# Two-layer transformer on one core: attention in float32 row strips, with q and k moved to their strips by one transfer per head and chunk, in place of stacked bfloat16 parts read back from DRAM

## The reference

```python
# layer 0: q, k, v: [16 heads, 2048, 8]; q and k are rotated (rope); k and v come from a latent of 32
q = apply_rope(q); k = apply_rope(k)
scores = jnp.einsum('bhqd,bhkd->bhqk', q, k) / jnp.sqrt(jnp.float32(HEAD_DIM))
scores = jnp.where(causal[None, None], scores, -jnp.inf)
attn = jax.nn.softmax(scores, axis=-1)
out = jnp.einsum('bhqk,bhkd->bhqd', attn, v)
```

## Time and profile before

| | us |
|---|---|
| median of 3 runs | 1527.86 |
| lowest and highest of them | 1524.72 and 4729.34 |
| span of the profiled execution | 1517.5 |
| attention, layer 0 | 109.8 to 605.3 |
| attention, layer 1 | 815.9 to 1308.3 |

### The profile page before, as it was taken

The page is one execution under the profiler, slowest core; times in us unless marked ns, Lnnn a source line. Parts: engine busy times, 40 slices in busy tenths (PEclk is TensorE's granted clock), DMA queues, the critical chain, the costliest instruction groups (busy, mean ns, idle before and its releaser), DMA issues. The chain is left out here.

```text
span 1517.5 us, 20983 instructions
## 1 busy us (share of the span) xinstructions
PE 1211.4 (80%) x7346; PEld 524.4 (35%) x7347; DVE 951.7 (63%) x2598; ACT 683.7 (45%) x895; POOL 187.9 (12%) x257
## 2 busy tenths in 40 slices
PE   2917999999799998319553899999989999676984
PEld 2502333333233343207421223233333334444663
DVE  6627888888678772301163788888868775342443
ACT  1302465665566666103230445566656667421331
POOL 4110000000000000344410000000000000054442
PEclk9857999999899999559875899999999999777997
DMA  4154000230502000022216310140120000011113
GB/s 128 31 118 68 16 16 15 39 74 16 67 15 73 3 3 1 22 63 57 76 50 123 52 43 19 35 87 25 26 44 2 3 3 2 1 35 43 47 47 104
DMA packets 41740, 64.10 MB, mean 42 GB/s; under 512 B 5440, under 2 KB 27872, under 8 KB 41328
## 3 DMA queue, kind: packets, MB, share of 16 engines
q1 hardware_dynamic: 37328, 53.95, 16.4%
q0 software_dynamic: 4320, 8.92, 1.7%
HBM read 45.55 MB, written 18.92 MB: 42 GB/s over the span
## 5 line engine op out<-in xcount | busy, mean ns | idle before, releaser
L792 ACT ACTIVATE probs_at<-st 128x1024 f32<-128x1024 f32 (+3 forms) x640 | 545.7, 897 | 382.4 <-PE st L747 236.4
L810 DVE TENSOR_REDUCE mxp_at<-mx 128x1 f32<-128x512 f32 x768 | 498.4, 685 | 96.0 <-PE mx L716 95.1
L716 PE MATMUL mx<-ks,qs 128*128 128x512 bf16 (+3 forms) x1280 | 379.9, 368 | 84.9 <-DVEq L801 33.2
L747 PE MATMUL st<-qs,ks 128*128 128x512 bf16 (+3 forms) x1280 | 355.6, 354 | 13.9 <-DMA qs<-shrow_at 12.6
L812 DVE CUSTOM_DVE_ANT_0 junk_at<-mx,maskN 128x384 f32<-128x384 f32 (+3 forms) x512 | 241.2, 485 | 104.7 <-PE mx L716 102.4
L763 PE MATMUL av<-probs_at,vs 128*32 128x512 f32 (+3 forms) x2560 | 301.7, 543 | 0.2
L716 PEld LDWEIGHTS mx<-ks,qs 128*128 128x128 bf16 x1280 | 104.8, 98 | 437.7 <-DVE mxp_at L810 183.6
L747 PEld LDWEIGHTS st<-qs,ks 128*128 128x128 bf16 x1280 | 123.4, 99 | 111.0 <-ACT probs_at L792 21.8
L1027 POOL DMA_INDIRECT perm<-rows,pos x64 | 63.3, 989 | 512.6 <-SPq L1136 248.4
L750 PE MATMUL st<-maskTb,identb 128*128 128x128 bf16 x512 | 100.9, 222 | 0.0
L763 PEld LDWEIGHTS av<-probs_at,vs 128*32 128x32 f32 x2560 | 50.6, 108 | 107.2 <-issue 96.7
(11 more groups left out here) (232 smaller groups left out, 1027.8 us busy)
## 6 DMA issues: line engine op xcount, KB each, us to landing
qs<-q_parts SPq DMA_DIRECT2D x63, 128.0 KB
ks<-k_parts SPq DMA_DIRECT2D x18, 384.0 KB
w_sb<-in_w_dram SPq DMA_DIRECT2D x16, 256.0 KB, 3.1
q_parts<-part_pj SPq DMA_DIRECT2D x12, 256.0 KB, 3.0
k_parts<-part_pj SPq DMA_DIRECT2D x12, 256.0 KB, 4.7
perm<-in_pad_dram SPq DMA_DIRECT2D x1, 2600.0 KB, 11.6
rows_f<-perm SPq DMA_DIRECT2D x39, 65.0 KB, 1.8
ks<-k_parts SPq DMA_DIRECT2D x12, 192.0 KB
```

The costliest lines, as they stand in the source:

```text
L716: pe.matmul(buf[:, 0:w], QS[p][:, j, (4 * Q + qb) * P:(4 * Q + qb + 1) * P], KS[p][:, j, c * CH:c * CH + w], start=True, stop=True).then_i ...
L747: mm = pe.matmul(st[half][:, y, off:CH], KS[p][:, j, kb * P:(kb + 1) * P], QS[p][:, j, Q * CH + off:(Q + 1) * CH], start=True, stop=True, ...
L792: act.activation(probs[:, s % 2, 2 * half:2 * half + 2, off:CH], st[half][:, :, off:CH], ACT.Exp, scale=SCALE).then_inc(exp_done[half], 1)
L810: ins = v.tensor_reduce(dst, buf[:, 0:w], AX.X, ALU.max)
```

## The change

- q and k stay float32. QT and KT hold all 16 heads: head 4g + j lies in partitions 32j to 32j + 7 of plane g. Partition 32j + 8 of KT holds ones, that of QT the shift. The split in three parts, the DRAM tensors, `load_q`, `load_k` and all waits on them are gone.
- `project` writes each chunk flat into qf (one operation in layer 1, by ScalarE for q and by VectorE for k; rope's last operation in layer 0). SP then issues, for each chunk and each of q and k, sixteen transfers of one head (8 partitions x 512 columns) from qf to the head's strip: 128 a layer. The block ends when all have landed.
- Maxima are float32 products over 8 rows and scores over 9 rows, each in the 32-row strip of its head (`tile_position=(32j, 0)`). The mask stays bfloat16 over the whole array and comes after both heads of a half.
- v goes straight into VS for all heads (copied by ScalarE in project); GpSimd's copies are gone.
- Probs has three buffers. The units come in another order, the maxima with the head innermost, each rotating buffer has a semaphore of its own. The copies of "turn" and "attT" go from VectorE to ScalarE; the shift is no longer split.
- The planner is new: it keeps a time per strip, charges w/1200 us for a product of w columns, and writes ScalarE's order too.

```diff
-UNITS = [(0, 0), (0, 1), (0, 2), (1, 1), (0, 3), (1, 2), (1, 3), (1, 0),
-         (2, 2), (2, 3), (3, 3), (2, 1), (3, 1), (2, 0), (3, 0), (3, 2)]
+UNITS = [(g, Q) for Q in (1, 0, 2, 3) for g in range(NG - 1)] + [(NG - 1, Q) for Q in (3, 2, 1, 0)]
...
-    return [(g, Q, j, qb, c) for qb in range(TPC) for j in range(GH) for c in range(Q + 1)]
+    return [(g, Q, j, qb, c) for qb in range(TPC) for c in range(Q + 1) for j in range(GH)]
...
+        found = []
+        if chores:
+            t, kind, x = min(chores)
+            found.append((max(pe, t, all_rows, free[b] + lat) - .2, "chore"))
+        if s < NST and ready[UNIT[s]] is not None and s < a + PB:
+            found.append((max(pe, ready[UNIT[s]] if STEPS[s][2] == 0 else 0., exp_done[half] + lat, rows[2 * half], rows[2 * half + 1]) - .1, "scores"))
+        if a < NST and probs_ready[a] is not None:
+            found.append((max(pe, probs_ready[a] + lat, all_rows, av_free + lat if STEPS[a][2] == 0 else 0.), "values"))
+        if k < len(maxes):
+            found.append((max(pe, rows[maxes[k][1][2]], free[b] + lat), "max"))
+        t, what = min(found)
+        if what == "max":
+            u, x = maxes[k]
+            w = max_width(x)
+            pe = max(t, pe) + .03
+            rows[x[2]] = pe + w / 1200
+            dve = max(dve, rows[x[2]] + lat) + .08 + w * .00104
...
+        elif what == "scores":
+            off = step_off(s)
+            pe = max(t + .1, pe) + .06
+            rows[2 * half] = rows[2 * half + 1] = done = pe + (CH - off) / 1200
+            if on_diagonal(s):
+                pe = done = max(rows) + .2
+                rows = [done] * GH
+            act = max(act, done + lat) + .05 + 2 * (CH - off) * .000833
...
+        elif what == "values":
+            pe = max(t, pe)
+            rows = [pe + (CH - step_off(a)) / 1200 + .05] * GH
...
                 for n, (i, c) in enumerate(steps):
...
+                    sp.wait_ge(flat_ready[i], s4 + c + 1)
+                    for h in range(H):
+                        g, j = divmod(h, GH)
+                        sp.dma_start((m.QT, m.KT)[i][RT * j:RT * j + HD, g, cols(c)], qf[i][h * HD:(h + 1) * HD, cols(c)]).then_inc(m.sem(f"heads_in{c}"), 16)
+                for c in range(NC4):
+                    sp.wait_ge(m.sem(f"heads_in{c}"), 16 * 2 * H * (L + 1))
...
-                        pe.matmul(buf[:, 0:w], QS[p][:, j, (4 * Q + qb) * P:(4 * Q + qb + 1) * P],
-                                  KS[p][:, j, c * CH:c * CH + w], start=True, stop=True).then_inc(mx_ready, 1)
+                        pe.matmul(buf[:, 0:w], QT[row(j, HD), g, (4 * Q + qb) * P:(4 * Q + qb + 1) * P], KT[row(j, HD), g, c * CH:c * CH + w],
+                                  start=True, stop=True, tile_position=(RT * j, 0)).then_inc(mx_ready, 1)
...
                         j = 2 * half + y
-                        mm = pe.matmul(st[half][:, y, off:CH], KS[p][:, j, kb * P:(kb + 1) * P], QS[p][:, j, Q * CH + off:(Q + 1) * CH],
-                                       start=True, stop=True, skip_group_check=diag)
-                        if diag:
+                        mm = pe.matmul(st[half][:, y, off:CH], KT[row(j, HD + 1), g, kb * P:(kb + 1) * P],
+                                       QT[row(j, HD + 1), g, Q * CH + off:(Q + 1) * CH], start=True, stop=True, tile_position=(RT * j, 0),
+                                       skip_group_check=on_diagonal(s))
+                    if on_diagonal(s):
+                        for y in range(2):
                             mm = pe.matmul(st[half][:, y, off:off + P], m.identb[:], m.maskTb[:], start=False, stop=True, skip_group_check=True)
                     mm.then_inc(st_ready[half], 1)
```

More of the change, by code:

```diff
@@ L73, in step_off, with on_diagonal @@
     return max(0, STEPS[s][2] * P - STEPS[s][1] * CH)
+def on_diagonal(s):
+    return STEPS[s][2] >= TPC * STEPS[s][1]
 def schedule():
[L79 to L95, removed]
+    maxes = [(u, m) for u, (g, Q) in enumerate(UNITS) for m in max_tiles(g, Q)]
+    last_max = [max(k for k, (x, _) in enumerate(maxes) if x == u) for u in range(NU)]
+    lat = .15
+    pe = dve = act = 0.
+    rows = [0.] * GH
+    free = [0.] * MXBUF
+    exp_done, probs_ready = [0., 0.], [None] * NST
+    ready, evacuated = [None] * NU, [None] * NU
@@ L96, in schedule @@
+    av_free = 0.
     normed = [0] * NC4
-    while k < len(base) or s < NST or norms:
+    chores = []
+    pe_order, act_order, rot = [], [], []
+    k = s = half = a = 0
+    while k < len(maxes) or s < NST or a < NST or chores:
         b = len(rot) % MXBUF
[L99 to L102, removed]
-            free[b] = dve
-            out.append(("rot", len(rot)))
-            rot.append((kind, x))
[L106 to L157, removed]
@@ L162 @@
+    return pe_order, act_order, rot, (pe, act, dve)
+PE_ORDER, ACT_ORDER, ROT, _ = schedule()
 NROT = len(ROT)
-ATTT_AT = {x: k for k, (kind, x) in enumerate(ROT) if kind == "attT"}
-NORM_AT = {x: k for k, (kind, x) in enumerate(ROT) if kind == "norm"}
+AT = {x: k for k, x in enumerate(ROT)}
+USES = [len(range(b, NROT, MXBUF)) for b in range(MXBUF)]
+TURN_NO = {x: n for n, x in enumerate(x for kind, x in ROT if kind == "turn")}
 class Count:
@@ L333, in project @@
         hT = sb("hT", [P, T])
-        qf, res = [sb(f"qf{i}", [P, CH]) for i in range(2)], [sb(f"res{i}", [P, CH]) for i in range(2)]
-        parts = [[sb(f"part{i}{a}", [P, T], BF) for a in range(3)] for i in range(2)]
+        qf = [sb(f"qf{i}", [P, T]) for i in range(2)]
         xn = sb("xn", [P, TILES, D])
@@ L728, in rotate @@
                         mm.then_inc(mx_ready, 1)
[L729 to L730 removed]
+                    else:
+                        pe.wait_ge(*released(AT["attT", x]))
                         for qb in range(TPC):
@@ L765, in values @@
                     mm.then_inc(av_done, 1)
-                for item in ORDER:
+                for item in PE_ORDER:
                     if item[0] == "rot":
                         rotate(item[1])
-                    elif item[0] == "av":
+                    elif item[0] == "values":
                         values(item[1])
                     else:
-                        _, s, half = item
-                        if STEPS[s][2] == 0 and half == 0:
-                            u = UNIT[s]
-                            pe.wait_ge(shift_set[u % 4], 16 * (L * (NU // 4) + u // 4 + 1))
-                        scores(s, half)
+                        scores(item[1], item[2])
@@ L779, in _, with exponent @@
             @block.scalar
             def _(act):
+                def exponent(s, half):
+                    off = step_off(s)
+                    if half == 0 and SB + s >= PB:
+                        act.wait_ge(av_done, SB + s - PB + 1)
+                    act.wait_ge(st_ready[half], SB + s + 1)
+                    act.activation(probs[:, s % PB, 2 * half:2 * half + 2, off:CH], st[half][:, :, off:CH], ACT.Exp,
+                                   scale=SCALE).then_inc(exp_done[half], 1)
@@ L1517, in layout @@
     ang = (np.arange(T, dtype=np.float32)[None, :] * inv[:, None]).astype(np.float32)
-    ones = np.zeros((GH, 2 * GH, T), np.dtype("bfloat16"))
-    for j in range(GH):
-        ones[j, 2 * j:2 * j + 2] = 1
     dw = np.zeros((E8 + 1, 3 * P, D), np.float32)
```

406 lines of the change are left out of this document (165 added, 241 removed).

## The result

The median of four runs is 2930.81 us (2929.24 to 2932.91); the kernel before has 1526.82 us beside it. The ratio is 1.919, with a 95% interval of 1.915 to 1.922. The forecast was 1746 us, its range ended at 2000. The sign was right and the size was not: the span of 2928.8 us is 1193 us longer than the 1735.5 us forecast for it.

A forecast was written before the change was run, and what follows sets the result against it. TensorE was taken to set the pace, VectorE close behind. Span 1517.5 us, plus 226 for two attentions (494 to 607 each), minus 8 for transfers, gives 1735.5; with 10.4 from span to median, 1746 us, range 1440 to 2000.

The forecast's parts named there:

- The clock: TensorE in attention: rival that 9-row products let the clock fall, doubling all; no own chance, counted within another rival's 0.12.
- The step: Attention, per layer: 112 steps of 3.15 us, 48 diagonal ones of 2.92, plus 99 and 15, giving 607 us.
- the wave: TensorE in attention: float32 products of 512 columns in separate row strips run together in 0.86 us.
- the mean of the orders: Attention steps: four strip-cycle positions average 3.58 us; the middle between 2.72 and 3.58, 3.15 us, was taken.
- the rival that they don't: TensorE in attention: row strips do not overlap or weight loads no longer hide; 2052 to 2860 us, chance 0.12.
- Its own upper case: Attention: upper end of the slower forecast's own range, 3.58 us a step and 3.2 a diagonal one, 1870 us.
- the lone maxima: Attention: planner's halved product cost leaves 26% of 640 maxima alone, 170 at VectorE's 0.58 us, 99 us a layer.
- The transfers: Before attention: 128 SP transfers a layer at 0.34 us, 43.5 us; attention 8 us earlier in layer 0, unchanged in layer 1.
- The bound of 0.62: SP's transfers before attention: upper price of 0.62 us each, 79 us a layer, +72 in all.
- the 3 us behind the last: Start of attention: 3 us for landing and barrier after SP's last transfer.
- the 10.4 us from span to median: Whole kernel: median of the runs lies 10.4 us above the profiled span, added to 1735.5 to give 1746.
- "slower": Whole kernel: forecast sign, slower than the kernel before, chance 0.71 against faster 0.15 and same 0.14.

The follow-up runs named there:

- half the transfers: Changed kernel contracting over all 32 rows of each strip, each SBUF transfer taking two chunks, 64 a layer in place of 128: 1970.37 us.
- run with 32 rows: Changed kernel with maxima and scores contracted over all 32 rows of their strip, added rows zeros times ones: 2062.93 us, ratio 1.341 to the kernel before.
- an even order: Changed kernel at 32 rows, planner replaced by a fixed order (both score halves, three maxima, values, one maximum): 2077.72 us, ratio 1.359.
- the measured price: Changed kernel at 32 rows, planner's cost of a product raised from w/1200 to w/600 us: 2137.36 us.

## Why the prediction was wrong

**The clock.** This is the step that failed. The rival was seen ("products of 9 rows might let the clock fall, doubling all of it") and then set aside within 0.12, on the ground that float32 products over 32 rows run at 1.00 in the projection. The earlier trace rows show that for 4 us which follow on products over the whole array (59.41 to 64.80); they say nothing of 1100 us of 8 and 9 rows. And the trace of before had the warning a few microseconds later, where products of the same kind, over 32 rows, went on:

```profile
72.00:74.00 2.00, 2.00 (x4) 0.58 (x3) 1.90 (x4) 0.19 (x2) 1.16 (x1) 0.50 0.00 0
74.00:76.00 2.00, 2.00 (x4) 0.58 (x2) 1.80 (x4) 1.15 (x2) 0.77 (x1) 0.50 0.70 201
...
73.03 1.94 PE L401 MATMUL st<-latT_pj,wukr 32*128 32x512 f32 x2
```

TensorE is busy for all of both rows and has 0.50. A wait of 1.06 us stands ahead of that stretch (before 69.86), so these rows alone don't tell rows from waits, but they took away the ground on which the rival was set aside. The rival's own words, doubled, would have given 607 x 2 = 1214 us a layer; 1162.65 came. Its place in the sum can be estimated: from the attention of 713.50 us at 0.92 (32 rows, half the transfers) and that of 1162.65 at 0.51, time against one over the clock gives (1162.65 - 713.50)/(1/0.51 - 1/0.92) = 514 us, and so 669 us for a layer at full clock. Two attentions that were not used for it lie within 7 us of that line (856.26 us at 0.74, 732.63 at 0.89). The clock is then, by this estimate, 494 us a layer, 987 of the 1193.

**The step.** 607 us a layer against 669 by that estimate: 62 too few, 124 in all. Two terms were too small, the wave and the mean of the orders. The run with 32 rows, at full clock, shows a step that is packed without loss, four scores, three maxima and the values:

```profile
543.63 1.07 PE L660 MATMUL av<-probs_at,vs 128*32 128x512 f32 x8
544.63 1.14 PE L644 MATMUL st<-qt,kt 32*128 32x512 f32 x8
545.59 1.03 PE L609 MATMUL mx<-kt,qt 32*128 32x512 f32 x6
546.55 1.06 PE L660 MATMUL av<-probs_at,vs 128*32 128x512 f32 x8
```

Eight passes one after another would be 3.44 us; here four products in four strips make room after 0.96 (544.63 to 545.59; the same in the run with half the transfers, 497.70 to 498.66). So row strips do run side by side, and the rival that they don't fell. But the wave is 0.96, not 0.86, and the packed step is 2.92, not 2.72: longer than the 2.78 of the kernel before, and with one maximum less. A step at these prices had nothing to win even at full clock. The Trainium skill ("TensorE: Matmul & The Clock Gate", "Part 3: Packing small matmuls") gave 1.12 us for a wave of four by the estimate in the prediction; the trace, with 0.96, lies between that and the forecast's 0.86, and the measurement decides. A short stretch of the changed kernel itself at full clock:

```profile
1258.12 1.06 PE L655 MATMUL av<-probs_at,vs 128*32 128x512 f32 x8
1259.11 1.13 PE L639 MATMUL st<-qt,kt 9*128 9x512 f32 x4
1260.17 0.28 PE L644 MATMUL st<-maskTb,identb 128*128 128x128 bf16 x2
```

Here two products in two strips take 1.06 us from their start to the mask's (1259.11 to 1260.17), with the change to the whole array for the mask in it. The values' 0.99 stands as in the earlier trace rows.

The mean of the orders was the other term. In the run with 32 rows the eight wide steps from the values at 538.22 to those at 566.51, all at a clock of 1.00, take between 2.05 and 5.41 us, 3.54 in the mean, against 3.15 forecast; the three with masks behind them (to 578.44) take 3.98, against 2.92. The prediction had followed its orders through and found 3.58, and then took off half of the way down to 2.72 because the planner knows strips; that discount was not there. Its own upper case, 3.58 and 3.2, is 669 a layer, the same as the estimate from the clock; to agree so closely is chance. The reason that it gave for the lone maxima, the planner's halved costs, was not confirmed: neither an even order nor the measured price shortened the layer.

**The lone maxima** were priced at 0.58 us, VectorE's pace. In the run of 32 rows that held while the clock was full (0.65 each at full width); at 0.50, where three buffers no longer outrun VectorE, three took 2.85, 0.95 each. A stretch that was only a small term of the sum costs the clock as well.

**The transfers.** 0.34 us each was read from the earlier trace rows, whose sources are in DRAM; from SBUF they take 0.67. 128 of them take 86 us, not 43.5; the first is issued at 48.29, earlier than the 55.05 forecast, and attention starts at 136.4 and not at 101.5. In layer 1 the way from the gather's issue to attention is 103.8 us (1443.87 to 1547.64) against 64.0. About 75 us of the miss in both layers. Better rows were at hand: the SP timeline of before has transfers from SBUF too, the parts on their way to DRAM (128 partitions each) and the shift,

```profile
81.11 1.83 SPq L380 DMA_DIRECT2D k_parts<-part_pj  x3
...
119.37 0.85 SPq L672 DMA_DIRECT2D qs<-shrow_at  x1
```

at 0.61 and 0.85 us each, and they were passed over. The bound of 0.62 was near the truth, +72 by the prediction's count. That no bytes limit it held, and so, nearly, did the 3 us behind the last (2.0).

**The rest** held, with one small exception: the 10.4 us from span to median came as 2.0. VectorE and ScalarE set no pace, their busy time in attention is what it was within some 10% (383 and 305 us against 381 and 280), and "slower" had 0.71. The range left out the clock, since that had been put among the strips that do not overlap, at the edge, and not as a case of its own with 1214 us a layer.

## What to carry to other kernels

Before taking rows away from TensorE's products, by strips or by a shorter contraction, look for the clock at which rows as thin run for long stretches; a packing that wins a few per cent of columns can lose a factor of two of clock, and zero rows that do nothing for the result took three tenths off the time here. Price a wave of packed products by a row that shows such waves: 0.96 for 0.86 was enough to turn a hoped-for gain of 2% in a step into a loss. Price a transfer by a row with the same kind of source, not only the same shape, and count transfers, not bytes. When a rival would double the largest term, give it a chance and a time of its own, however odd it looks.

## What the runs showed of the hardware

The clock fell while TensorE was busy without a gap. In the changed kernel it rose for some 14 us in layer 0, after products over all 128 rows (transposes from 1254.12 on, then masks between the scores), and fell again:

```profile
1255.00:1257.00 2.00, 2.00 (x13) 1.77 (x16) 0.12 (x1) 0.77 (x2) 0.00 (x0) 0.51 0.01 2
1257.00:1259.00 2.00, 2.00 (x18) 0.41 (x18) 1.90 (x10) 0.99 (x2) 0.00 (x0) 1.00 0.01 2
...
1269.00:1271.00 2.00, 2.00 (x10) 0.54 (x10) 0.00 (x0) 0.73 (x1) 0.00 (x0) 0.90 0.04 8
1271.00:1273.00 2.00, 2.00 (x14) 0.75 (x14) 0.00 (x0) 1.19 (x2) 0.00 (x0) 0.50 0.00 0
```

All four rows have TensorE busy for all of their 2.00 us. The Trainium skill ("TensorE: Matmul & The Clock Gate", "Part 1: The HAM clock gate") has the gate follow how busy TensorE has recently been. Busy for 1149.87 of 1162.65 us and granted 0.51, this kernel doesn't agree with that taken as time without gaps; the measurement decides.

Zeros times ones in the added rows were enough to bring the clock back, so it was not the values in them that counted. A transfer of 8 partitions cost SP 0.34 us from DRAM; from SBUF it cost 0.672 with 512 columns and 0.675 with 1024. Four float32 products of 512 columns in four row strips held TensorE for 0.96 us at full clock.
